# Second attention of a gated two-layer block: the output bias added by a TensorE product instead of a GpSimd addition, and GpSimd's small factor product in front of its rounding

## The chip, the cores and the metric

The kernel runs on one core of one Trainium2 chip. The metric is the device time of one execution in microseconds. Before the change three runs gave 405.77, 406.14 and 408.43 us, a median of 406.14 us. Engines are called by the profile's names: PE is TensorE (PEld its weight load), DVE is VectorE, ACT is ScalarE, POOL is GpSimd, SP is SyncE, which issues the DMAs.

## The reference, cut to what matters

The whole block has two layers, each a cross attention and a feed-forward part, each behind a normalisation and a gate:

```
x = x + tanh(g_xattn[0]) * L0_xattn(ctx, norm(x), mask, ...)
x = x + tanh(g_ffn[0])   * L0_ffn(norm(x), ...)        # 16 experts, top-k tokens
x = x + tanh(g_xattn[1]) * L1_xattn(norm(x), ctx, ctx, ...)
x = x + tanh(g_ffn[1])   * L1_ffn(norm(x), ...)        # ternary weights, 8-bit activations
```

The change lies in the last two lines. With 32 sequences of 64 rows and 128 channels, they compute

```
wq, wk, wv = q @ wq_w.T + wq_b, k @ wk_w.T + wk_b, v @ wv_w.T + wv_b   # 16 heads of 8
probs = softmax(wq . wk / sqrt(8));  attn = probs . wv
y = attn @ wo_w.T + wo_b                                 # wo_b: the bias that moves
x = x + tanh(g) * y
h = layernorm(x) * gamma + beta
scale = 127 / max(|h|);  hq = round(h * scale)           # act_quant, a row at a time
u = (hq @ w1q.T) / (scale * sw) + b1;  g = gelu(u)       # then the same again with w2, b2
```

The gate is already folded into the prepared weight and bias, so the kernel only has to add `attn @ w + bias` to x. The bias wo_b is a row of 128 numbers that is the same for all tokens.

## The kernel before, in words

The tokens are 2048 rows, cut into 16 tiles (t = 0 to 15) of 128 rows by 128 channels, float32; the tile with x is `xs[:, t, :]`. The function `attention_ffn` computes the second layer for all 16 tiles, and its work starts where the first layer's experts end. Each engine has its own queue, strictly in the written order, and the engines meet only at semaphores. So the order of the work is written out by hand, engine by engine: first a short loop that adds the expert outputs up, then a loop over steps s in which every engine treats several tiles at once, each at another stage, and then a hand-ordered tail for the last tiles and the second half of the feed-forward part.

In a turn of the loop PE does, in this order, for different tiles: `mix` (probabilities by values, 8 small products in each of two halves, j=1 into bank `b_y` and j=0 into bank `b_m`, L1533), `turn_context` (L1474), `turn_attention` (transposes the divided attention rows, L1545), `turn_input` (L1480), `up` (first feed-forward product, L1566), `scores` (L1504), `turn_norm` (L1559), `probs_T` (eight transposes, L1519), `out_proj` (attention rows by output weight, into `b_y`, L1550) and `project` (query, key, value, L1490 to L1493).

DVE does `row_stats` (L1896), `norm_largest` (L1905), `attend` (reciprocal of the sums L1878, then the two products into `b_att`, L1883), `norm_factors` (L1910 gives the bound, semaphore h_bound; L1913 its reciprocal, semaphore h_fine), `row_moments` (L1900), `hidden` (L1920), `row_max` (L1861), `output` (L1892: x is set to the product in `b_y` plus `xb`), `shift` (L1866) and `invert` (L1874).

POOL does `add_bias` (L1352: `xb` = x + bias, x and bias both in SBUF), `norm_round` (L1374: multiplies by the fine factor and rounds, waits for h_fine), `norm_back` (L1380: a 128x1 product that keeps the factor back to full scale, waits for h_bound), `normalise` (L1339), `inverse_root` (L1356, L1359), `norm` (L1366 to L1369) and `spread_keys` (L1346). In the tail POOL also does `add_bias_2` (L1387) and `hidden_back` (L1393), DVE `hidden_largest` (L1925), `hidden_bound` (L1930) and `hidden_round` (L1939).

ACT moves PSUM results to SBUF (`b_oT` L1727 is the transposed attention that out_proj reads) and does the exponential (L1717) and the gelu (L1737). In the profile the names of tiles carry the prefix b_.

Of the kernel before, what the change touches and what calls it, by code (L numbers as in the profile page):

```python
# [22 lines left out]
ALU = mybir.AluOpType  # L23
# [7 lines left out]
P = 128  # L31


def wait(eng, sem, count):

    if isinstance(count, int) and count <= 0:
        return
    eng.wait_ge(sem, count)
# [27 lines left out]
def exists(t, tiles):  # L66

    return not isinstance(t, int) or 0 <= t < tiles
# [1169 lines left out]
def attention_ffn(nc, v, o_tiles):  # L1238
# [6 lines left out]
    xs, cs, mrow, nrow, neghalf, ident, quad = (v[n] for n in "xs cs mrow nrow neghalf ident quad".split())  # L1245
# [12 lines left out]
    with ExitStack() as ph, nc.Block() as block:  # L1258
        def sb(name, shape, dt=F32):
            return ph.enter_context(nc.sbuf_tensor("b_" + name, shape, dt))  # L1260
# [4 lines left out]
        def sem(name):  # L1265
# [14 lines left out]
        rs = sb("rs", [P, 2, HP, 2])  # L1280
        att = sb("att", [P, 2, HP, 2, DH])
        oT = sb("oT", [P, 2, P])
        xb = sb("xb", [P, 2, D])
        hn = sb("hn", [P, 2, D])
        hr = sb("hr", [P, 2, D])
        hT = sb("hT", [P, 2, P], BF16)
# [17 lines left out]
        p_prob, p_mix, p_out = (p_m, p_t), (p_m, p_y), (p_t, p_m)  # L1304
        (zeroed, ready, xn_ready, cT_done, xT_done, cT_ready, xT_ready, qkv_done, k_ready, q_ready, v_ready, k4_ready,
         scored, maxed, shifted, exped, pT_done, prT_ready, mixed, inverse, att_ready, aT_done, oT_ready, y_done,
         xb_ready, x_new) = (
            sem(n) for n in ("zeroed", "ready", "xn_ready", "cT_done", "xT_done", "cT_ready", "xT_ready", "qkv_done",
                             "k_ready", "q_ready", "v_ready", "k4_ready", "scored", "maxed", "shifted", "exped",
                             "pT_done", "prT_ready", "mixed", "inverse", "att_ready", "aT_done", "oT_ready", "y_done",  # L1310
                             "xb_ready", "x_new"))
        (stats_ready, mv_ready, var_ready, rstd_ready, hn_chain, hn_ready, h_max, h_bound, h_fine, h_back, hr_ready,
         hT_done, hT_ready, up_done, hid_ready, gelu_done, g_max, g_bound, g_fine, g_back, g_rounded, gT_done,
         gT_ready, down_done, xb2_ready, x_done) = (
# [13 lines left out]
        @block.sync  # L1328
        def _(sp):
            for t in range(NT // 2):  # L1330
                sp.wait_ge(x_done, t + 1)
                sp.dma_start(o_tiles[:, 2 * t:2 * t + 2, :], xs[:, 2 * t:2 * t + 2, :]).then_inc(stored, 16)
            sp.wait_ge(stored, 16 * (NT // 2))

        @block.gpsimd
        def _(pool):
# [5 lines left out]
            def spread_keys(t, tp):  # L1342
# [3 lines left out]
                    last = nc.gpsimd.tensor_tensor(k4[:, tp, b], ksb[:, tp, b].unsqueeze(1).to_broadcast([P, G, S]),  # L1346
                                                   quad[:].unsqueeze(2).to_broadcast([P, G, S]), ALU.mult)
                last.then_inc(k4_ready, 1)

            def add_bias(t, tp):  # L1350
                wait(pool, x_new, t - 1)
                nc.gpsimd.tensor_tensor(xb[:, tp, :], xs[:, t, :], rows[:, 2, :], ALU.add).then_inc(xb_ready, 1)  # L1352

            def inverse_root(t):
                pool.wait_ge(mv_ready, t + 1)
                nc.gpsimd.tensor_tensor(nrow[:, t, :], mrow[:, t, 0:4:2], mrow[:, t, 1:4:2], ALU.subtract)\  # L1356
                    .then_inc(var_ready, 1)
                pool.wait_ge(var_ready, t + 1)
                nc.gpsimd.tensor_tensor(nrow[:, t, 1:2], nrow[:, t, 1:2], neghalf[:, 0:1], ALU.pow)\  # L1359
                    .then_inc(rstd_ready, 1)  # L1360

            def norm(t, tp):
                pool.wait_ge(rstd_ready, t + 1)
                wait(pool, hr_ready, t - 1)
                step = Steps(pool, hn_chain, 2 * t)
                step(nc.gpsimd.tensor_scalar(hn[:, tp, :], xs[:, t, :], nrow[:, t, 0:1], nrow[:, t, 1:2],  # L1366
                                             ALU.add, ALU.mult))
                step(nc.gpsimd.tensor_tensor(hn[:, tp, :], hn[:, tp, :], rows[:, 4, :], ALU.mult))
                nc.gpsimd.tensor_tensor(hn[:, tp, :], hn[:, tp, :], rows[:, 5, :], ALU.add).then_inc(hn_ready, 1)  # L1369

            def norm_round(t, tp):
                pool.wait_ge(h_fine, t + 1)
                wait(pool, hT_done, t - 1)
                nc.gpsimd.tensor_scalar(hr[:, tp, :], hn[:, tp, :], fine[:, 0, t % 4], MAGIC, ALU.mult, ALU.add)\  # L1374
                    .then_inc(hr_ready, 1)

            def norm_back(t):
                pool.wait_ge(h_bound, t + 1)
                wait(pool, hid_ready, t - 3)
                nc.gpsimd.tensor_tensor(back_[:, 0, t % 4], top[:, 0, t % 4], wback[:, 0:1], ALU.mult).then_inc(h_back, 1)  # L1380
# [9 lines left out]
            def hidden_back(j):  # L1390
                pool.wait_ge(g_bound, j + 1)
                r = slice(2 * j, 2 * j + 2)
                nc.gpsimd.tensor_tensor(back2[:, r], top2[:, r], wback[:, 1:2].to_broadcast([P, 2]),  # L1393
                                        ALU.mult).then_inc(g_back, 1)
# [8 lines left out]
            pool.wait_ge(ready, 1)  # L1403
            pool.wait_ge(rooted, NT)
            for s in range(NT + 1):
                if exists(s - 3, NT):
                    add_bias(s - 3, (s - 3) % 2)
                if exists(s - 5, NT):
                    norm_round(s - 5, (s - 5) % 2)
                    norm_back(s - 5)  # L1410
                if exists(s + 3, NT):
                    normalise(s + 3)
                if exists(s - 4, NT):
                    inverse_root(s - 4)
                    norm(s - 4, s % 2)
                if s >= 1 and exists(s, NT):
                    spread_keys(s, s % 2)
            inverse_root(13)
            add_bias(14, 0)
            norm(13, 1)  # L1420
            norm_round(12, 0)
            norm_back(12)
            add_bias(15, 1)
            add_bias_2(0)
            inverse_root(14)
            norm_round(13, 1)
            norm_back(13)
            norm(14, 0)
            add_bias_2(1)
            hidden_back(0)  # L1430
# [3 lines left out]
            inverse_root(15)  # L1434
            add_bias_2(4)
            norm(15, 1)
            norm_round(14, 0)
            norm_back(14)
            add_bias_2(5)
            hidden_back(2)  # L1440
            add_bias_2(6)
            hidden_back(3)
            add_bias_2(7)
            hidden_back(4)
            norm_round(15, 1)
            norm_back(15)
            hidden_back(5)
            hidden_back(6)
            hidden_back(7)
# [2 lines left out]
        def _(pe):  # L1452
# [94 lines left out]
            def out_proj(t, tp):  # L1547
                pe.wait_ge(oT_ready, t + 1)
                wait(pe, hid_ready, t - 2)
                nc.tensor.matmul(p_y[:, 0:D], oT[:, tp, :], w_c[:, 3, :], start=True, stop=True).then_inc(y_done, 1)  # L1550

            def turn_norm(t, tp):
                pe.wait_ge(hr_ready, t + 1)
# [266 lines left out]

        @block.vector
        def _(dve):
            nc.vector.memset(vals[:], 0.0).then_inc(zeroed, 1)
            nc.vector.tensor_copy(wback[:, 0:1], wmean[:, 0:1])
            nc.vector.tensor_scalar(wback[:, 1:2], wmean[:, 1:2], gates[:, 3:4], None, ALU.mult).then_inc(ready, 1)
            dve.wait_ge(zeroed, 1)
            for a in range(2):
                nc.vector.memset(vals[a * S:(a + 1) * S, :, :, :, a, DH:DH + 1].rearrange("p x b n o -> p (x b n) o"), 1.0)\
                    .then_inc(zeroed, 1)
# [58 lines left out]

            def output(t, tp):
                dve.wait_ge(y_done, t + 1)  # L1890
                dve.wait_ge(xb_ready, t + 1)
                nc.vector.tensor_tensor(xs[:, t, :], p_y[:, 0:D], xb[:, tp, :], ALU.add).then_inc(x_new, 1)  # L1892

            def row_stats(t, tp):
                dve.wait_ge(x_new, t + 1)
# [171 lines left out]
```

## Time and profile before

| | before |
|---|---|
| median of 3 runs (lowest to highest) | 406.14 us (405.77 to 408.43) |
| profiled execution: its own time | 406.96 us |
| its span, first to last instruction | 404.5 us |
| mean granted TensorE clock | 0.97 of full speed |
| busy: PE, PEld, DVE, ACT, POOL | 371.9, 274.4, 323.2, 258.3, 221.4 us |
| the second layer's loop over tiles | about 286 to 371 us of the span |
| the hand-ordered tail | about 371 us to the end |

The profiled execution took 2.5 us more than its span, and 0.8 us more than the median of the runs. A float32 product of 128x128 by 128x128 stands in the trace as two matmul records, a float32 transpose as one. Matmul records overlap, so what a product costs a busy PE is read from start to start and not from the duration of one record. A few records of L1566 are missing from the trace; where they are, PE shows a gap called "issue".

### The profile page before, as it was taken

The numbers are of one execution on the slowest core, as the hardware profiler recorded it, in microseconds if no ns is written. First come the engines' busy times: TensorE is split into PE (matmuls) and PEld (weight loads), VectorE is DVE, ScalarE is ACT, GpSimd is POOL, SyncE is SP. The second block draws the span as 40 slices with busy tenths as digits, with TensorE's granted clock in tenths as the row PEclk, the third lists the DMA queues.
The fourth block names the chain that finished last, engine by engine and source line by source line (L and its number), as shares of the span: only waits on it lengthen the run. The fifth ranks groups of instructions, "written<-read, shape, count | busy, mean of one in ns | idle before, by whom it ended". The sixth has DMA issues, their size and how long they took to land. (4 is left out here: it accounts for less than half of the span.)

```text
span 404.5 us, 10543 instructions
## 1 busy us (share of the span) xinstructions
PE 371.9 (92%) x3599; PEld 274.4 (68%) x3612; DVE 323.2 (80%) x911; ACT 258.3 (64%) x514; POOL 221.4 (55%) x388
## 2 busy tenths in 40 slices
PE   7799999999999999999999999999799888886675
PEld 7356766676666666678756888787577777765464
DVE  4889999899989989888482888464647888887896
ACT  2578767777777777776654222345357777777784
POOL 4574577766666666663231000076438888877760
PEclk9999999999999999999999999999769999999689
DMA  5979999900000000000000000000000000000003
GB/s 152 258 145 115 138 128 125 93 2 2 2 2 1 2 2 2 2 0 5 0 2 0 2 0 2 1 2 2 0 2 2 2 2 4 2 2 2 2 13 92
DMA packets 61283, 13.27 MB, mean 33 GB/s; under 512 B 51488, under 2 KB 60592, under 8 KB 61232
## 3 DMA queue, kind: packets, MB, share of 16 engines
q1 hardware_dynamic: 59776, 11.94, 21.4%
q10 hardware_dynamic: 1328, 0.66, 0.6%
q8 instruction: 30, 0.49, 0.5%
q14 instruction: 21, 0.17, 0.2%
q0 software_dynamic: 128, 0.00, 0.0%
HBM read 11.55 MB, written 1.05 MB: 31 GB/s over the span
## 5 line engine op out<-in xcount | busy, mean ns | idle before, releaser
L398 POOL TENSOR_TENSOR a_rn<-a_ssq,neghalf 128x8 f32<-128x8 f32 x48 | 79.0, 1655 | 29.1 <-DVE a_ssq L999 24.5
L999 DVE TENSOR_REDUCE a_ssq<-q_home 128x8 f32<-128x512 f32 x48 | 32.3, 673 | 6.5 <-ACT q_home L784 6.4
L90 POOL TENSOR_TENSOR nrow<-mrow 128x2 f32<-128x2 f32 x32 | 6.3, 198 | 55.8 <-DVE mrow L86 55.5
L487 PE MATMUL a_x<-wkv_a,a_kvT 128*128 128x512 f32 x64 | 34.5, 621 | 0.9 <-ACT kv_home L790 0.8
L790 ACT ACTIVATE kv_home<-a_x,maskcol 128x512 f32<-128x512 f32 x32 | 21.9, 684 | 18.4 <-PE a_x L487 18.4
L1346 POOL TENSOR_TENSOR b_k<-b_ksb,quad 128x256 f32<-128x256 f32 x32 | 19.0, 614 | 15.5 <-ACT b_ksb L1697 15.5
L1861 DVE TENSOR_REDUCE b_mx<-b_s 128x16 f32<-128x1024 f32 x16 | 19.6, 1224 | 6.3 <-PE b_s L1504 6.3
L414 POOL TENSOR_TENSOR a_yr<-a_ymv,eps_row 128x1 f32<-128x1 f32 x16 | 3.1, 191 | 37.8 <-DVE a_ymv L1042 37.8
L1018 DVE TENSOR_REDUCE a_mx<-a_s 128x4 f32<-128x512 f32 x32 | 21.9, 685 | 2.0 <-PE a_s L513 1.9
L802 ACT ACTIVATE kv_home<-a_m,cols 128x512 f32<-128x512 f32 x32 | 22.0, 686 | 0.8 <-PE a_m L501 0.6
L532 PE MATMUL a_m<-kv_home,p_home 128*64 128x65 f32 x512 | 22.0, 228 | 0.3 <-ACT p_home L812 0.3
L513 PEld LDWEIGHTS a_s<-kv_home,q_home 64*64 64x64 f32 x512 | 13.9, 132 | 12.1 <-issue 12.1
L1025 DVE TENSOR_TENSOR p_home<-a_s,a_mx 128x512 f32<-128x512 f32 x32 | 21.8, 682 | 0.0
L523 PEld LDWEIGHTS a_m<-ident,p_home 128*128 128x128 f32 x128 | 14.6, 140 | 10.2 <-issue 10.0
L501 PEld LDWEIGHTS a_m<-ident,q_home 128*128 128x128 f32 x128 | 15.3, 140 | 9.2 <-issue 7.9
L532 PEld LDWEIGHTS a_m<-kv_home,p_home 128*64 128x64 f32 x512 | 17.7, 137 | 5.5 <-issue 5.5
L812 ACT COPY p_home<-a_m 128x512 f32<-128x512 f32 x32 | 18.7, 586 | 4.0 <-PE a_m L523 4.0
L551 PEld LDWEIGHTS a_y<-wo_a,p_home 128*128 128x128 f32 x128 | 16.6, 191 | 6.4 <-issue 6.2
L92 POOL TENSOR_TENSOR nrow<-nrow,neghalf 128x1 f32<-128x1 f32 x32 | 18.8, 588 | 2.5
L523 PE MATMUL a_m<-ident,p_home 128*128 128x128 f32 x128 | 20.1, 280 | 0.0
L807 ACT ACTIVATE p_home<-p_home 128x512 f32<-128x512 f32 x32 | 19.9, 622 | 0.3 <-DVE p_home L1025 0.3
L501 PE MATMUL a_m<-ident,q_home 128*128 128x128 f32 x128 | 19.3, 273 | 0.4 <-DVE q_home L1011 0.4
(294 smaller groups left out, 1150.7 us busy)
## 6 DMA issues: line engine op xcount, KB each, us to landing
w_gu<-in_L_ffn_Wg_dram SPq DMA_DIRECT2D x4, 512.0 KB, 9.2
w_gu<-in_L_ffn_Wu_dram SPq DMA_DIRECT2D x4, 512.0 KB, 11.2
w_d<-in_L_ffn_Wd_dram SPq DMA_DIRECT2D x8, 256.0 KB, 8.5
out_dram<-xs SPq DMA_DIRECT2D x8, 128.0 KB, 1.8
xs<-in_x_dram SPq DMA_DIRECT2D x1, 640.0 KB, 11.2
cs<-in_ctx_dram SPq DMA_DIRECT2D x1, 640.0 KB, 11.2
wkv_a<-in_L_xattn_Wkv_dram SPq DMA_DIRECT2D x1, 512.0 KB, 7.5
nat<-in_L_ffn_w_dram SPq DMA_DIRECT2D x2, 256.0 KB, 3.1
```

The source lines that it names most:

```text
L398: nc.gpsimd.tensor_tensor(rn[:, tp, i, :], ssq[:, tp, i, :], neghalf[:, 0:H0], ALU.pow)\
L487: nc.tensor.matmul(p_x[:], kvT[:, tp, b * 2 * S:(b + 1) * 2 * S], wkv_a[:, INNER:2 * INNER], start=True, stop=True).then_inc(vproj_done, 1)
L501: last = nc.tensor.transpose(p_m[b][:, h * P:(h + 1) * P], kn[:, b, h * P:(h + 1) * P], ident[:])
L523: last = nc.tensor.transpose(p_m[a][:, h * P:(h + 1) * P], pr[:, a, h, :], ident[:])
L532: last = nc.tensor.matmul(p_m[a][b * S:(b + 1) * S, h * W:(h + 1) * W], prT[:, a, h, b * S:(b + 1) * S], vaug[:, tp, b, 2 * h + a, :], sta ...
L790: nc.scalar.activation(vaug[:, tp, b, :, 0:DH0], p_x[:].rearrange("p (h d) -> p h d", h=H0), ACT.Copy, scale=maskcol[:, 2 * t + b:2 * t + ...
L802: nc.scalar.activation(kT[:, tp, b, :, :], p_m[b][:].rearrange("p (h k) -> p h k", h=HP), ACT.Copy, scale=cols[:, 4:5]).then_inc(kT_ready, 1)
L807: nc.scalar.activation(pr[:, a], pr[:, a], ACT.Exp).then_inc(exped, 1)
L999: nc.vector.tensor_reduce(ssq[:, tp, i, :], sq[:, i, :].rearrange("p (h d) -> p h d", h=H0), AX.X, ALU.add).then_inc(reduced, 1)
L1018: nc.vector.tensor_reduce(mx[:, a, :], p_s[a][:].rearrange("p (h k) -> p h k", h=HP), AX.X, ALU.max)\
L1025: nc.vector.tensor_tensor(pr[:, a], s3, mx[:, a, :].unsqueeze(2).to_broadcast([P, HP, P]), ALU.subtract).then_inc(shifted, 1)
L1861: nc.vector.tensor_reduce(mx[:, tp], s4, AX.X, ALU.max).then_inc(maxed, 1)
```

## The change

Four things change, all in `attention_ffn`.

`out_proj` issues two products into the same bank instead of one. The first multiplies a constant tile `first_row` (128x128, ones in its first row and zeros elsewhere) by the tile that holds the bias in every row, and so writes the bias to all 128 rows; the second is the old product and is added on top (start=False).

`add_bias` and its tile `xb`, its semaphore xb_ready and its 16 calls on POOL are gone. DVE's `output` adds the bank to x in place and waits for one semaphore less.

On POOL `norm_back` stands in front of `norm_round` of the same tile, in the loop and in the tail.

DVE fills `first_row` by two memsets at the start of `attention_ffn`.

```diff
@@ -1280,7 +1280,7 @@
         rs = sb("rs", [P, 2, HP, 2])
         att = sb("att", [P, 2, HP, 2, DH])
         oT = sb("oT", [P, 2, P])
-        xb = sb("xb", [P, 2, D])
+        first_row = sb("first_row", [P, P])
         hn = sb("hn", [P, 2, D])
         hr = sb("hr", [P, 2, D])
         hT = sb("hT", [P, 2, P], BF16)
@@ -1304,11 +1304,11 @@
         p_prob, p_mix, p_out = (p_m, p_t), (p_m, p_y), (p_t, p_m)
         (zeroed, ready, xn_ready, cT_done, xT_done, cT_ready, xT_ready, qkv_done, k_ready, q_ready, v_ready, k4_ready,
          scored, maxed, shifted, exped, pT_done, prT_ready, mixed, inverse, att_ready, aT_done, oT_ready, y_done,
-         xb_ready, x_new) = (
+         x_new) = (
             sem(n) for n in ("zeroed", "ready", "xn_ready", "cT_done", "xT_done", "cT_ready", "xT_ready", "qkv_done",
                              "k_ready", "q_ready", "v_ready", "k4_ready", "scored", "maxed", "shifted", "exped",
                              "pT_done", "prT_ready", "mixed", "inverse", "att_ready", "aT_done", "oT_ready", "y_done",
-                             "xb_ready", "x_new"))
+                             "x_new"))
         (stats_ready, mv_ready, var_ready, rstd_ready, hn_chain, hn_ready, h_max, h_bound, h_fine, h_back, hr_ready,
          hT_done, hT_ready, up_done, hid_ready, gelu_done, g_max, g_bound, g_fine, g_back, g_rounded, gT_done,
          gT_ready, down_done, xb2_ready, x_done) = (
@@ -1346,10 +1346,6 @@
                     last = nc.gpsimd.tensor_tensor(k4[:, tp, b], ksb[:, tp, b].unsqueeze(1).to_broadcast([P, G, S]),
                                                    quad[:].unsqueeze(2).to_broadcast([P, G, S]), ALU.mult)
                 last.then_inc(k4_ready, 1)
-
-            def add_bias(t, tp):
-                wait(pool, x_new, t - 1)
-                nc.gpsimd.tensor_tensor(xb[:, tp, :], xs[:, t, :], rows[:, 2, :], ALU.add).then_inc(xb_ready, 1)
 
             def inverse_root(t):
                 pool.wait_ge(mv_ready, t + 1)
@@ -1403,11 +1399,9 @@
             pool.wait_ge(ready, 1)
             pool.wait_ge(rooted, NT)
             for s in range(NT + 1):
-                if exists(s - 3, NT):
-                    add_bias(s - 3, (s - 3) % 2)
                 if exists(s - 5, NT):
+                    norm_back(s - 5)
                     norm_round(s - 5, (s - 5) % 2)
-                    norm_back(s - 5)
                 if exists(s + 3, NT):
                     normalise(s + 3)
                 if exists(s - 4, NT):
@@ -1416,15 +1410,13 @@
                 if s >= 1 and exists(s, NT):
                     spread_keys(s, s % 2)
             inverse_root(13)
-            add_bias(14, 0)
             norm(13, 1)
+            norm_back(12)
             norm_round(12, 0)
-            norm_back(12)
-            add_bias(15, 1)
             add_bias_2(0)
             inverse_root(14)
+            norm_back(13)
             norm_round(13, 1)
-            norm_back(13)
             norm(14, 0)
             add_bias_2(1)
             hidden_back(0)
@@ -1434,16 +1426,16 @@
             inverse_root(15)
             add_bias_2(4)
             norm(15, 1)
+            norm_back(14)
             norm_round(14, 0)
-            norm_back(14)
             add_bias_2(5)
             hidden_back(2)
             add_bias_2(6)
             hidden_back(3)
             add_bias_2(7)
             hidden_back(4)
+            norm_back(15)
             norm_round(15, 1)
-            norm_back(15)
             hidden_back(5)
             hidden_back(6)
             hidden_back(7)
@@ -1547,7 +1539,8 @@
             def out_proj(t, tp):
                 pe.wait_ge(oT_ready, t + 1)
                 wait(pe, hid_ready, t - 2)
-                nc.tensor.matmul(p_y[:, 0:D], oT[:, tp, :], w_c[:, 3, :], start=True, stop=True).then_inc(y_done, 1)
+                nc.tensor.matmul(p_y[:, 0:D], first_row[:], rows[:, 2, :], start=True, stop=False)
+                nc.tensor.matmul(p_y[:, 0:D], oT[:, tp, :], w_c[:, 3, :], start=False, stop=True).then_inc(y_done, 1)
 
             def turn_norm(t, tp):
                 pe.wait_ge(hr_ready, t + 1)
@@ -1820,10 +1813,12 @@
 
         @block.vector
         def _(dve):
+            nc.vector.memset(first_row[:], 0.0)
             nc.vector.memset(vals[:], 0.0).then_inc(zeroed, 1)
             nc.vector.tensor_copy(wback[:, 0:1], wmean[:, 0:1])
             nc.vector.tensor_scalar(wback[:, 1:2], wmean[:, 1:2], gates[:, 3:4], None, ALU.mult).then_inc(ready, 1)
             dve.wait_ge(zeroed, 1)
+            nc.vector.memset(first_row[0:1, :], 1.0)
             for a in range(2):
                 nc.vector.memset(vals[a * S:(a + 1) * S, :, :, :, a, DH:DH + 1].rearrange("p x b n o -> p (x b n) o"), 1.0)\
                     .then_inc(zeroed, 1)
@@ -1888,8 +1883,7 @@
 
             def output(t, tp):
                 dve.wait_ge(y_done, t + 1)
-                dve.wait_ge(xb_ready, t + 1)
-                nc.vector.tensor_tensor(xs[:, t, :], p_y[:, 0:D], xb[:, tp, :], ALU.add).then_inc(x_new, 1)
+                nc.vector.tensor_tensor(xs[:, t, :], p_y[:, 0:D], xs[:, t, :], ALU.add).then_inc(x_new, 1)
 
             def row_stats(t, tp):
                 dve.wait_ge(x_new, t + 1)
```

PE, one turn of the loop around out_proj, before (b_oT is the transposed attention, w_c the weights, b_k, b_y, b_m and b_t PSUM banks):

```order
L1519 MATMUL b_m<-ident,b_pr 128x128 x3
L1550 MATMUL b_y<-w_c,b_oT 128x128 [waits b_hid_ready,b_oT_ready]
L1490 MATMUL b_k<-b_cT,w_c 128x128 [waits b_k_ready,b_oT_ready,b_q_ready,b_hT_ready,b_v_ready,b_xT_ready,b_cT_ready]
L1491 MATMUL b_k<-b_xT,w_c 128x128
L1493 MATMUL b_k<-w_c,b_cT 128x128 x2
L1533 MATMUL b_y<-b_vals,b_prT 64x18 [waits b_hid_ready,b_x_new,b_att_ready,b_v_ready,b_prT_ready]
```

PE at the same place, now:

```order
L1511 MATMUL b_m<-ident,b_pr 128x128 x3
L1542 MATMUL b_y<-rows,b_first_row 128x128 [waits b_hid_ready,b_oT_ready]
L1543 MATMUL b_y<-w_c,b_oT 128x128
L1482 MATMUL b_k<-b_cT,w_c 128x128 [waits b_k_ready,b_oT_ready,b_q_ready,b_hT_ready,b_v_ready,b_xT_ready,b_cT_ready]
L1483 MATMUL b_k<-b_xT,w_c 128x128
L1485 MATMUL b_k<-w_c,b_cT 128x128 x2
L1525 MATMUL b_y<-b_vals,b_prT 64x18 [waits b_hid_ready,b_x_new,b_att_ready,b_v_ready,b_prT_ready]
```

One product more stands between the transposes of the probabilities and the projections, and the two waits of out_proj now stand in front of the new product.

POOL, one turn of the loop, before:

```order
L1346 TENSOR_TENSOR b_k<-b_ksb,quad 128x256
L1352 TENSOR_TENSOR b_xb<-xs,rows 128x128 [waits b_x_new]
L1374 TENSOR_SCALAR b_hr<-b_hn,b_fine 128x128 [waits b_hT_done,b_h_fine]
L1380 TENSOR_TENSOR b_back_<-b_top,b_wback 128x1 [waits b_hid_ready,b_h_bound]
L1339 TENSOR_SCALAR b_xn<-xs,nrow 128x128 [waits b_xT_done]
L1356 TENSOR_TENSOR nrow<-mrow 128x2 [waits b_mv_ready]
```

POOL at the same place, now:

```order
L1346 TENSOR_TENSOR b_k<-b_ksb,quad 128x256
L1376 TENSOR_TENSOR b_back_<-b_top,b_wback 128x1 [waits b_hid_ready,b_h_bound]
L1370 TENSOR_SCALAR b_hr<-b_hn,b_fine 128x128 [waits b_hT_done,b_h_fine]
L1339 TENSOR_SCALAR b_xn<-xs,nrow 128x128 [waits b_xT_done]
L1352 TENSOR_TENSOR nrow<-mrow 128x2 [waits b_mv_ready]
```

The addition into b_xb is gone (in the new numbering L1352 is another line), and the 128x1 product stands ahead of the rounding.

## Rows read from the trace of the kernel before

**Rows 1.** The page, part 1: busy time of each engine, share of the span, instructions.

```profile
PE 371.9 (92%) x3599; PEld 274.4 (68%) x3612; DVE 323.2 (80%) x911; ACT 258.3 (64%) x514; POOL 221.4 (55%) x388
```

**Rows 2.** Timeline of PE, one turn (start us, us, instruction, idle before).

```profile
329.07 0.33 PE L1545 MATMUL b_k<-ident,b_att 128*128 128x128 f32 x1 [0.44 <-DVE b_att L1883]
...
331.36 0.39 PE L1550 MATMUL b_y<-w_c,b_oT 128*128 128x128 f32 x2
331.58 0.39 PE L1490 MATMUL b_k<-b_cT,w_c 128*128 128x128 f32 x2
...
332.57 0.65 PE L1533 MATMUL b_y<-b_vals,b_prT 128*64 128x18 f32 x16
333.06 0.63 PE L1533 MATMUL b_m<-b_vals,b_prT 128*64 128x18 f32 x16
...
334.38 0.33 PE L1545 MATMUL b_k<-ident,b_att 128*128 128x128 f32 x1 [0.44 <-DVE b_att L1883]
```

**Rows 3.** Timeline of DVE, the same turn.

```profile
330.50 1.22 DVE L1861 TENSOR_REDUCE b_mx<-b_s 128x16 f32<-128x1024 f32 x1
331.79 0.29 DVE L1892 TENSOR_TENSOR xs<-b_y,b_xb 128x128 f32<-128x128 f32 x1
331.99 1.21 DVE L1866 TENSOR_TENSOR b_pr<-b_s,b_mx 128x1024 f32<-128x1024 f32 x1
333.26 0.21 DVE L1874 RECIPROCAL b_rs<-b_y 128x8 f32<-128x8 f32 x1
...
333.55 0.27 DVE L1905 TENSOR_REDUCE b_top<-b_hn 128x1 f32<-128x128 f32 x1
333.73 0.21 DVE L1878 RECIPROCAL b_rs<-b_m 128x8 f32<-128x8 f32 x1
...
334.25 0.14 DVE L1910 TENSOR_SCALAR b_top<-b_top 128x1 f32<-128x1 f32 x1
```

**Rows 4.** Chain of waits: out_proj of the first tile (start us, us, what).

```profile
299.21 0.43 PE b_y L1550 x2
```

**Rows 5.** Timeline of PE, summing the expert outputs: two products added into one bank.

```profile
262.38 0.61 PE L1463 MATMUL b_s<-ws_t,kv_home 128*128 128x128 f32 x4
262.92 0.44 PE L1467 MATMUL b_s<-b_turned 128*64 128x128 f32 x4
```

**Rows 6.** Timeline of POOL, the same turn of the loop.

```profile
333.12 1.18 POOL L1346 TENSOR_TENSOR b_k<-b_ksb,quad 128x256 f32<-128x256 f32 x2 [0.36 <-ACT b_ksb L1697]
334.26 0.45 POOL L1352 TENSOR_TENSOR b_xb<-xs,rows 128x128 f32<-128x128 f32 x1
334.70 0.37 POOL L1374 TENSOR_SCALAR b_hr<-b_hn,b_fine 128x128 f32<-128x128 f32 x1
```

**Rows 7.** Timeline of all engines in the tail, about the last two tiles.

```profile
376.34 0.46 POOL L1352 TENSOR_TENSOR b_xb<-xs,rows 128x128 f32<-128x128 f32 x1
...
380.35 0.77 PE L1550 MATMUL b_y<-w_c,b_oT 128*128 128x128 f32 x2 [0.31 <-DVE b_hid L1920]
...
381.07 1.60 POOL L1387 TENSOR_TENSOR xs<-xs,rows 128x256 f32<-128x256 f32 x2
381.24 0.28 DVE L1892 TENSOR_TENSOR xs<-b_y,b_xb 128x128 f32<-128x128 f32 x1
381.44 0.64 DVE L1939 TENSOR_SCALAR b_hid<-b_hid,b_fine 128x512 f32<-128x512 f32 x1
...
382.21 0.49 DVE L1930 TENSOR_SCALAR b_top<-b_top 128x2 f32<-128x2 f32 x1
...
382.70 0.13 DVE L1930 TENSOR_SCALAR b_top<-b_top 128x2 f32<-128x2 f32 x1
```

**Rows 8.** A stretch: us, busy time (count) of PE, PEld, DVE, ACT, POOL, granted clock, DMA, GB/s.

```profile
286.00:302.00 16.00, 13.47 (x125) 10.88 (x127) 7.05 (x11) 8.29 (x22) 4.68 (x10) 0.57 0.01 2
```

**Rows 9.** Timeline of PE: the same instruction of two early turns.

```profile
295.53 0.48 PE L1545 MATMUL b_k<-ident,b_att 128*128 128x128 f32 x1 [0.29 <-DVE b_att L1883]
...
303.10 0.33 PE L1545 MATMUL b_k<-ident,b_att 128*128 128x128 f32 x1 [0.44 <-DVE b_att L1883]
```

## The prediction, before the changed kernel had run

> **What bounds the kernel now.** I read the page first: PE is busy for 92% of the span, DVE for 80%, POOL for 55% [rows 1]. That points at PE, but a share over the whole span doesn't say what an added PE product costs in the one loop where it is added. So I read the timeline of a single turn of that loop, engine by engine, and the chain of waits beside it.
>
> A turn lasts 5.31 us: `turn_attention` starts at 329.07 and again at 334.38 [rows 2]. PE has work without a hole from the scores to the end of the two halves of `mix`; what it waits for is 0.44 us each turn, always for DVE's `b_att`. So the turn closes like this: PE ends mix, DVE divides (L1878, L1883), PE transposes the result, and PE goes on through scores, transposes, out_proj, projections and mix again.
>
> Is it PE or DVE that sets the pace in that ring? DVE shows almost no idle time there either, so I compare starts with ends. The record of out_proj ends at 331.36 + 0.39 = 331.75 and DVE's `output` starts at 331.79. The first half of mix ends at 332.57 + 0.65 = 333.22 and `invert` starts at 333.26. The second half ends at 333.06 + 0.63 = 333.69 and the next reciprocal starts at 333.73 [rows 2, 3]. Three times DVE starts exactly 0.04 us behind PE. Two of these starts lie later than DVE's own queue would put them: `row_max` ended at 331.72 and `shift` at 333.20, so `output` and `invert` came 0.07 and 0.06 us after the end of what stood before, while a DVE instruction that waits for nothing starts before the recorded end of the one ahead of it (333.55 + 0.27 = 333.82, next start 333.73) [rows 3]. DVE therefore waits for PE, by little (0.07 + 0.09, some 0.16 us at `output`, and about as much again at `invert`). PE sets the pace, and a longer PE turn is a longer turn.
>
> **The added product, in the loop.** A 128x128 float32 product costs a busy PE its distance from start to start: out_proj starts at 331.36 and the next product at 331.58, 0.22 us [rows 2]. (Its two records last 0.39 together because they overlap the next.) The new product has the same shape, and it stands in the continuous part. That it adds into the same bank costs no extra by the nearest rows: four records that add into one bank went from 262.38 to 262.92, 0.54 us [rows 5], and the four records of the projections that don't take the same time in front of 332.57. The loop runs out_proj for tiles 0 to 13. Thirteen of them run at the full clock: 13 x 0.22 = 2.9 us. Tile 0 falls into the stretch at a mean granted clock of 0.57 [rows 8], that is mostly at the lower level, and its product cost 0.43 us on the chain [rows 4]: +0.43. (If the clock rises at the same moment as before, only about 0.22 of it is left, since work pushed past that moment runs fast.) Loop: +3.3 us. The ends: nothing, if PE isn't what binds (the first rival), and 14 x 0.39 = 5.5 us, if the new product cost the whole recorded length of the old one. I take 0.22, since the very same product stands in that row.
>
> **The removed addition on POOL.** 16 x 0.46 us = 7.3 us of POOL's work go [rows 6]. In the loop they stand between `spread_keys` and `norm_round`. POOL is idle there for 0.36 us a turn, waiting for ACT's keys, which come from PE's projections [rows 6], so POOL is not what the turn waits for. The 0.46 us become idle time: 0 gained.
>
> **The swap on POOL.** `norm_back` now waits first, for the bound, which DVE finishes at 334.25 + 0.14 = 334.39 [rows 3]. Before, the addition covered that wait. The 128x1 product behind it is a short one, and the rounding, which starts at 334.70 now [rows 6], has 0.3 us of room for it. So with the cover gone the rounding is not delayed, and nothing is gained. What queues behind is `normalise`, which is needed only in the next turn: 0. DVE's `output` reads x instead of xb, with one wait less and the same shape: 0. Two memsets at the start of the part have 128 columns each, like the 0.29 us of `output`, so 0.6 us at most, and DVE waits for PE's first sum behind them: 0.
>
> **The tail.** Tile 14's product is hidden, since PE waits for ACT before and after it and DVE is in a long reduction meanwhile. Tile 15's isn't. It runs at the lower clock (its pair took 0.77 us against 0.39 [rows 2, 7]), where a product costs 0.43 [rows 4]; the old one ended at about 381.1, the new pair at 381.55, and DVE's `output`, now at 381.24, moves to 381.6: +0.35, and everything behind it on DVE. Against this stands a stall in the same place. DVE's L1930 on 128x2 takes 0.13 us at 382.70 but 0.49 at 382.21, when it ends at 382.70 just as POOL's two additions do at 381.07 + 1.60 = 382.67; L1939 at 381.44 ends at 382.08, 0.2 us after the first of them [rows 7]. The Trainium skill, "SBUF — State Buffer" (section "SBUF: two separate sides"), says that a DVE instruction in a two-port mode and a GpSimd instruction hold one port pair as an exclusive lock, so that the loser waits for the whole instruction; these rows agree. With the addition at 376.34 gone, POOL's queue, which is full from there on, comes 0.41 us earlier (the next instruction stood 0.41 behind it), and its last addition ends at 382.26. DVE, 0.35 later, then finds POOL done at L1930 and saves those 0.35 us, but L1939 now meets POOL's second addition and ends at about 382.45. From 382.70 the sequence is 0 to 0.1 us later than before: **tail +0.1**, between -0.5 and +0.6, since each further meeting of the two engines can cost or save 0.2 to 0.5.
>
> **Sum.** 0.43 + 2.9 + 0.1 = +3.4 us. The profiled execution (span 404.5, its own time 406.96) would become 410.4; it lies 0.8 above the median of the runs, so the forecast against the median of 406.14 is **409.5 us**, 0.8% slower.
>
> **Rivals.**
>
> *DVE sets the pace (not slower), chance 0.12.* If the ends of PE's records, which the profile models, are late by 0.2 us, DVE's queue binds the turn and the new product falls into PE's waiting time of 0.44 us. It decides from 0.22 us of slack in `row_max` to `invert`. Then only tile 0 and the tail show: 406.1 + 0.4 at most, and with a better meeting with POOL in the tail (-0.5) 405.9. For it: DVE has hardly a gap of 0.1 us in those rows. Against: three starts that follow PE by the same 0.04 us. The skill's port rule would favour this rival, as 0.46 us of POOL's two-input additions go each turn; but in the loop L1910 stands right beside L1352 and takes 0.14 us [rows 3, 6], its undisturbed time, so there is nothing to save.
>
> *The product costs more than its spacing (slower), chance 0.07.* Its own weights, loaded each turn, and a bank that is still being written could break the stream. At its whole recorded length of 0.39 a turn: 406.1 + 5.5 + 0.1 = 411.7. Against: the 0.54 us of four records, adding or not [rows 5].
>
> *The clock (slower), chance 0.12.* TensorE is at its lower level of 1.2 GHz in most of 286 to 302 [rows 8] and again in the tail, where tile 15's pair ran [rows 7], each time after PE had stood waiting for other engines. Nothing in front of 286 changes, so the first fall stays; when it rises again, and where the second fall meets a tail that begins 3.3 us later, can shift. One turn more at 1.2 GHz costs as much as the difference between the turn from 295.53 to 303.10 and a full-speed one, 7.6 - 5.3 = 2.3 us [rows 2, 9]: 411.8. The Trainium skill, "TensorE: Matmul & The Clock Gate" (Part 4), says that transposes don't count as activity for this gate. By that rule the added product, which is no transpose, could only help to keep the clock up; no run here shows yet that it does, and I give it no time.
>
> *As forecast, chance 0.69*, with its own range of 408.7 to 410.5: 0.2 for the first tile, 0.5 for the tail, 0.3 for the medians.
>
> **Range and chances.** The forecast and part of the clock case below 411.2, and from the first rival's side down to 407.3, hold 8 in 10: **407.3 to 411.2**. This kernel's runs tell a difference from none at about 1%, here 4.1 us, so the border to "slower" is 410.2 and to "faster" 402.1. Slower by over 1%: 0.07, most of the clock case (0.10) and some of the forecast's (0.08): 0.25. Faster by over 1%: 0.01. Within 1%: 0.74.
>
> **What would show it.** In the new trace the turn should be 5.53 us, with the two products of out_proj 0.22 apart, `output` still 0.04 behind the second one's end, and PE's wait for `b_att` still 0.44. POOL's wait for ACT's keys should grow from 0.36 to about 0.9, since it loses 0.46 and the turn grows. A turn of 5.31 with a wait of 0.22 on PE would prove the first rival, a product spacing over 0.3 the second, a stretch of half clock longer than before the third. The forecast is wrong in the tail if DVE's L1930 at the old 382.21 still takes 0.4 us or more.

## The result: slower by 0.6%, and the profile after

In 20 runs each the changed kernel takes 406.66 us (406.11 to 410.44) and the one before 405.51 (402.62 to 408.43). The ratio is **1.0064, 95% interval 1.0045 to 1.0083**, that is +2.6 us (1.8 to 3.4) on 405.5. The forecast was +3.4 us on a median of 406.14, 409.5 us. That median of three was itself 0.6 above the one of 20 runs; the measured ratio on it gives 1.0064 x 406.14 = 408.7 us, inside the range of 407.3 to 411.2. As a difference, +2.6 stands against +3.4. The two medians as they stand lie closer together, 1.15 us or 1.0028, and 406.66 by itself is below the range: single executions of either kernel scatter by more than the change (the lowest and highest of the kernel before are 5.8 us apart), and the ratio, taken run by run in their order, is the figure that has an interval.

The page of the profile after, busy time and granted clock:

```profile
PE 376.0 (93%) x3644; PEld 277.1 (69%) x3644; DVE 323.5 (80%) x913; ACT 257.8 (64%) x514; POOL 215.1 (53%) x372
...
PEclk9999999999999999999999999999899999998599
```

PE has 4.1 us more than before and POOL 6.3 less, with 16 instructions fewer [rows 1]. The span is 404.5 us, the same as before to a tenth. Read alone, that would say that the change costs nothing. A turn of the loop says otherwise. PE in the changed kernel (start us, us, instruction, idle before), the turn that answers to [rows 2]:

```profile
332.43 0.33 PE L1537 MATMUL b_k<-ident,b_att 128*128 128x128 f32 x1 [0.44 <-DVE b_att L1878]
...
334.72 0.39 PE L1542 MATMUL b_y<-rows,b_first_row 128*128 128x128 f32 x2
334.94 0.39 PE L1543 MATMUL b_y<-w_c,b_oT 128*128 128x128 f32 x2
335.17 0.39 PE L1482 MATMUL b_k<-b_cT,w_c 128*128 128x128 f32 x2
...
336.15 0.65 PE L1525 MATMUL b_y<-b_vals,b_prT 128*64 128x18 f32 x16
336.64 0.63 PE L1525 MATMUL b_m<-b_vals,b_prT 128*64 128x18 f32 x16
...
337.96 0.33 PE L1537 MATMUL b_k<-ident,b_att 128*128 128x128 f32 x1 [0.44 <-DVE b_att L1878]
```

337.96 - 332.43 is 5.53 us, against 5.31. From `turn_attention` to out_proj 2.29 us pass in both kernels (331.36 - 329.07 before); the two products stand 0.22 apart, the projection behind them is 0.45 later than the start of the first instead of 0.22, and the wait for `b_att` is still 0.44. The whole product has gone into the turn. DVE in the same turn:

```profile
335.37 0.29 DVE L1886 TENSOR_TENSOR xs<-b_y,xs 128x128 f32<-128x128 f32 x1 [0.28 <-PE b_y L1543]
335.57 1.21 DVE L1861 TENSOR_TENSOR b_pr<-b_s,b_mx 128x1024 f32<-128x1024 f32 x1
336.85 0.21 DVE L1869 RECIPROCAL b_rs<-b_y 128x8 f32<-128x8 f32 x1
...
337.32 0.20 DVE L1873 RECIPROCAL b_rs<-b_m 128x8 f32<-128x8 f32 x1
```

`output` starts 0.04 us behind the end of the second product (334.94 + 0.39 = 335.33), `invert` 0.05 and its second part 0.05 behind the halves of mix. The releases of [rows 3] are the same, but in front of `output` DVE now shows 0.28 us idle: more slack, as it must be where PE sets the pace. POOL, answering to [rows 6]:

```profile
336.70 1.18 POOL L1346 TENSOR_TENSOR b_k<-b_ksb,quad 128x256 f32<-128x256 f32 x2 [0.77 <-ACT b_ksb L1690]
338.05 0.19 POOL L1376 TENSOR_TENSOR b_back_<-b_top,b_wback 128x1 f32<-128x1 f32 x1 [0.16 <-DVE b_top L1904]
338.28 0.37 POOL L1370 TENSOR_SCALAR b_hr<-b_hn,b_fine 128x128 f32<-128x128 f32 x1
```

Its wait for the keys went from 0.36 to 0.77, with 0.16 more in front of `norm_back`, where the addition used to stand. The rounding starts 0.32 us after `turn_attention` (338.28 - 337.96), exactly as before (334.70 - 334.38).

**Why the spans are equal.** I set the starts of `turn_attention` of both profiles beside each other:

| stretch | before | after | difference |
|---|---|---|---|
| start of the span to tile 0's | 295.53 | 294.55 | -0.98 |
| first turn | 7.57 | 5.16 | -2.41 |
| the next 12 turns | 63.48 | 66.19 | +2.71 |
| tile 13's to tile 15's | 11.96 | 12.64 | +0.68 |
| from there to the end | 25.96 | 25.96 | 0.00 |

The first two lines aren't the change's, all but the 0.22 us that tile 0's product adds to the first turn: in front of 286 us the program is unchanged but for two memsets, and the granted clock of the stretch differs (0.50 from 288 to 300 us before, 0.73 and 0.84 in 288 to 292 and 292 to 296 after, then 1.00). The same window as [rows 8], of the kernel after (us, busy time and count of PE, PEld, DVE, ACT, POOL, granted clock, DMA, GB/s), and its two early turns, as in [rows 9]:

```profile
286.00:302.00 16.00, 12.76 (x169) 10.31 (x168) 9.53 (x18) 11.18 (x29) 7.16 (x15) 0.89 0.01 2
```

```profile
294.55 0.33 PE L1537 MATMUL b_k<-ident,b_att 128*128 128x128 f32 x1 [0.45 <-DVE b_att L1878]
...
299.71 0.33 PE L1537 MATMUL b_k<-ident,b_att 128*128 128x128 f32 x1 [0.44 <-DVE b_att L1878]
```

The one profiled execution of the kernel before had an unlucky stretch at half clock there, 0.57 against 0.89, and one first turn of 7.57 us that the eight other profiles show as 4.7 to 5.4. Those 3.4 us hide the 3.4 us of the loop and the last tiles. The fourth line has tile 13's product and the second fall of the clock, at about 372 us after and 377 before. The other profiles part the two: the same stretch takes 11.96, 12.05 and 12.04 us in the three kernels without an added product, 12.18 in the kernel with a zero product and in the changed kernel profiled again, and 12.40 with two zero products. So about 0.2 of the 0.68 is the product, and the rest belongs to this one execution.

### The profile page after: what moved, and what is told of

Same layout as the page of the kernel before. It is cut to its first block and busy times, and to the rows that moved or that the text cites. A ratio compares the mean times of both kernels' runs of the same rounds, so it can differ in the third digit from the quotient of the medians.

```text
span 404.5 us, 10590 instructions
## 1 busy us (share of the span) xinstructions
PE 376.0 (93%) x3644; PEld 277.1 (69%) x3644; DVE 323.5 (80%) x913; ACT 257.8 (64%) x514; POOL 215.1 (53%) x372
```

## Experiments

Theory P: PE sets the pace of the loop, a product in its continuous part costs its start-to-start distance, and what POOL does costs nothing. Rivals: the cost comes from the operand or bank and not from the place (the whole record), from the swap on POOL, or DVE sets the pace. All but the last kernel ran in five rounds with the kernel before beside them. The first four shared one chip (kernel before 404.8 us), the other three another (404.4).

### One zero product, POOL as before

`zero_row` is a 128x128 tile of zeros, filled once by DVE, so the product adds nothing to the result.

```diff
-  nc.tensor.matmul(p_y[:, 0:D], oT[:, tp, :], w_c[:, 3, :], start=True, stop=True).then_inc(y_done, 1)
+  nc.tensor.matmul(p_y[:, 0:D], zero_row[:], rows[:, 2, :], start=True, stop=False)
+  nc.tensor.matmul(p_y[:, 0:D], oT[:, tp, :], w_c[:, 3, :], start=False, stop=True).then_inc(y_done, 1)
```

> The kernel before with one more product in out_proj: a tile of zeros by the bias tile, added into the same bank; GpSimd keeps its addition, its order and its own time. Theory (PE sets the turn, the product is the whole price): the turn goes from 5.31-5.32 to 5.54 us, +0.22 in each of 13 turns plus the two slow tiles, in all +3.0 to +3.6 us over the kernel before, ratio 1.007 to 1.009. Rival 1 (DVE sets the turn, the product falls into PE's wait): turn 5.32, ratio 1.000 to 1.001. Rival 2 (the removal on GpSimd gives part back in the changed kernel): this kernel is slower than the changed one by 0.3 us or more.

Measured: 406.49 us, ratio 1.0056 (1.0024 to 1.0087). The ratio came out below the 1.007 to 1.009 that I had expected, but its interval reaches into that range. PE of this kernel:

```profile
331.00 0.33 PE L1546 MATMUL b_k<-ident,b_att 128*128 128x128 f32 x1 [0.44 <-DVE b_att L1886]
...
333.30 0.39 PE L1551 MATMUL b_y<-rows,b_zero_row 128*128 128x128 f32 x2
333.52 0.39 PE L1552 MATMUL b_y<-w_c,b_oT 128*128 128x128 f32 x2
...
336.55 0.33 PE L1546 MATMUL b_k<-ident,b_att 128*128 128x128 f32 x1 [0.44 <-DVE b_att L1886]
```

5.55 us a turn, the changed kernel's to a hundredth or two, with all of POOL's additions still there. The product alone makes the loop's loss. The ratios can't say whether this kernel is slower than the changed one by a few tenths of a microsecond, as the rival of the removal on POOL asked: the interval here alone is 1.3 us wide to each side. The turns say that nothing of it is in the loop; the tail follows below.

### Two zero products

The same edit with the zero product twice.

> The same with two added zero products. PE sets the turn: turn 5.76 us, twice the difference of the kernel with one (+6 to +7 us, ratio 1.015 to 1.017). If part of the first product had been covered by slack, the second one costs more than the first; if the product costs only where the queue stalls, both cost less than 0.22 a turn.

Measured: 410.66 us, ratio 1.0156 (1.0113 to 1.0198), which is +6.3 us. Its PE:

```profile
330.15 0.33 PE L1546 MATMUL b_k<-ident,b_att 128*128 128x128 f32 x1 [0.44 <-DVE b_att L1887]
...
332.44 0.39 PE L1551 MATMUL b_y<-rows,b_zero_row 128*128 128x128 f32 x2
332.67 0.39 PE L1552 MATMUL b_y<-rows,b_zero_row 128*128 128x128 f32 x2
332.89 0.39 PE L1553 MATMUL b_y<-w_c,b_oT 128*128 128x128 f32 x2
...
335.91 0.33 PE L1546 MATMUL b_k<-ident,b_att 128*128 128x128 f32 x1 [0.44 <-DVE b_att L1887]
```

The turn is 5.76, again 0.22 more, and twelve turns take 68.95 us: 5.47 over the 63.48 of before, 2 x 12 x 0.228. With 0.44 each for tiles 0 and 13 that makes 6.35 us, what the ratio says. The cost of a turn grows in proportion from the first product, so there was no slack that the first one used up.

### The changed kernel without its bias product

The output bias is left out: POOL doesn't add it, and PE has no product for it.

```diff
-  nc.tensor.matmul(p_y[:, 0:D], first_row[:], rows[:, 2, :], start=True, stop=False)
-  nc.tensor.matmul(p_y[:, 0:D], oT[:, tp, :], w_c[:, 3, :], start=False, stop=True).then_inc(y_done, 1)
+  nc.tensor.matmul(p_y[:, 0:D], oT[:, tp, :], w_c[:, 3, :], start=True, stop=True).then_inc(y_done, 1)
```

> The changed kernel without its first product in out_proj, so the output bias of the second attention is left out; GpSimd's addition is gone and its order swapped. Theory: GpSimd isn't waited for in the loop, so the turn stays 5.31-5.32 us and GpSimd's wait for the keys grows from 0.36 to about 0.8; only the tail can move, by -0.5 to +0.1 us: ratio 0.998 to 1.000. Rival (GpSimd's two-input additions hold up DVE in the loop): turn 5.2 us or less, ratio below 0.996.

Measured: 403.03 us, ratio 0.9986 (0.9955 to 1.0016). PE, then POOL:

```profile
331.08 0.33 PE L1537 MATMUL b_k<-ident,b_att 128*128 128x128 f32 x1 [0.44 <-DVE b_att L1877]
...
336.40 0.33 PE L1537 MATMUL b_k<-ident,b_att 128*128 128x128 f32 x1 [0.44 <-DVE b_att L1877]
```

```profile
335.14 1.18 POOL L1346 TENSOR_TENSOR b_k<-b_ksb,quad 128x256 f32<-128x256 f32 x2 [0.54 <-ACT b_ksb L1689]
```

The turn is back at 5.32 us. Taking 0.46 us a turn off POOL gives a turn nothing; it turns up as waiting time: 0.54 here and 0.16 in front of `norm_back`, together 0.70 against 0.36, where I had expected about 0.8 in one place.

### The kernel before with the swap alone

```diff
-  norm_round(s - 5, (s - 5) % 2)
   norm_back(s - 5)
+  norm_round(s - 5, (s - 5) % 2)
```

(and so for tiles 12 to 15 in the tail)

> The kernel before with GpSimd's small factor product in front of the rounding, nothing else. Theory: the addition in front still covers the wait, so the rounding starts about 0.15 us later (behind the product) and has 0.3 us of room or more before PE turns it: turn 5.31-5.32, ratio 0.999 to 1.001. Rival: PE's transposition of the rounded rows waits, turn 5.4 or more, ratio 1.002 or more.

Measured: 404.27 us, ratio 1.0005 (0.9975 to 1.0035). POOL of this kernel, whose `turn_attention` stands at 332.50:

```profile
332.38 0.45 POOL L1352 TENSOR_TENSOR b_xb<-xs,rows 128x128 f32<-128x128 f32 x1
332.80 0.19 POOL L1380 TENSOR_TENSOR b_back_<-b_top,b_wback 128x1 f32<-128x1 f32 x1
332.96 0.37 POOL L1374 TENSOR_SCALAR b_hr<-b_hn,b_fine 128x128 f32<-128x128 f32 x1
```

The rounding starts 0.46 after `turn_attention` and so 0.14 later than before, since here the addition still stands in front. The next `turn_attention` is at 337.81, a turn of 5.31: the delay is absorbed. In the changed kernel it doesn't even arise.

### The same product in PE's wait instead

If P holds, PE's 0.44 us of waiting for `b_att` would take both products (2 x 0.22) for nothing. They need another bank there, since `b_y` holds the sums of mix at that time: 128 columns of `b_s` behind the scores are free between DVE's `shift` and the next scores. DVE's `output` and `row_stats` follow behind `attend`. Tiles 0 to 12 go this way, 13 to 15 the old one. PE's waits move with them: out_proj waits for DVE's `shift`, the next scores that go into the same bank wait for `output`, and `up` and `mix` of the early tiles no longer do. The core of the edit, against the changed kernel:

```diff
+  EARLY = NT - 3
+  def y_out(t):
+      return p_s[:, 0, 4 * S:4 * S + D] if t < EARLY else p_y[:, 0:D]
...
   if s >= 2 and exists(s, NT):
       turn_context(s)
+  if exists(s - 4, NT):
+      out_proj(s - 4, s % 2)
   if exists(s - 3, NT):
       turn_attention(s - 3, (s - 3) % 2)
...
-  if exists(s - 3, NT):
+  if s - 3 == EARLY:
       out_proj(s - 3, (s - 3) % 2)
...
   attend(s - 2, s % 2)
+  output(s - 3, (s - 3) % 2)
   norm_factors(s - 4)
+  row_stats(s - 3, (s - 3) % 2)
```

> The changed kernel with both products of out_proj taken out of PE's continuous part for tiles 0 to 12: they go into PE's wait for the divided attention rows, right behind the next tile's mix, and write into unused columns of a scores bank; DVE's addition and the row statistics move behind the division, where DVE waits for the up product. Theory (a product costs 0.22 us a turn only where PE has no hole; PE still sets the turn): the wait of 0.44 us takes both products (0.44), the turn falls from 5.54 to 5.10 us, 4 to 5.5 us less than the changed kernel and 1.5 to 3 less than the kernel before: ratio 0.992 to 0.996. Rival (DVE, which has 0.46 us of waiting in a turn and now does the same work in another order, becomes the bound): turn 5.3 or more, ratio 1.000 or more.

Measured: **400.96 us, ratio 0.9925 (0.9894 to 0.9956)**, faster than both kernels (the changed one takes 406.5 on this chip, below). PE, then DVE:

```profile
328.51 0.39 PE L1553 MATMUL b_s<-rows,b_first_row 128*128 128x128 f32 x2
328.73 0.39 PE L1554 MATMUL b_s<-w_c,b_oT 128*128 128x128 f32 x2
329.11 0.33 PE L1545 MATMUL b_k<-ident,b_att 128*128 128x128 f32 x1
...
334.15 0.33 PE L1545 MATMUL b_k<-ident,b_att 128*128 128x128 f32 x1
```

```profile
329.15 0.29 DVE L1900 TENSOR_TENSOR xs<-b_s,xs 128x128 f32<-128x128 f32 x1
```

A turn is 5.04 us and no wait is left in front of L1545, which still starts 0.69 us behind the end of mix, as before: PE does the two products while DVE divides. From 319.03 to 359.36 there are eight such turns, in which PE is busy for 39.11 of 40.33 us.

### The same place, bias added by POOL

The same edit on the kernel before, so one product in the wait and POOL's addition kept.

> The kernel before (bias added by GpSimd) with its one product of out_proj moved in the same way. Theory: turn 5.10 us as well, since the hole has room for one product or two; ratio 0.991 to 0.995, no different from the version with two products by more than 0.2%. If the hole is too small for two, this one is faster by up to 0.22 us a turn (2.6 us). Rival (DVE bound): 5.3 or more, ratio 1.000 or more.

Measured: 401.08 us, ratio 0.9925 (0.9891 to 0.9959).

```profile
328.03 0.39 PE L1561 MATMUL b_s<-w_c,b_oT 128*128 128x128 f32 x2
328.63 0.33 PE L1553 MATMUL b_k<-ident,b_att 128*128 128x128 f32 x1 [0.22 <-DVE b_att L1897]
...
333.76 0.33 PE L1553 MATMUL b_k<-ident,b_att 128*128 128x128 f32 x1 [0.22 <-DVE b_att L1897]
```

Here half of the wait is left, 0.22 us, which is the room that the bias product fills in the kernel above; the medians differ by 0.1 us. So the same product that costs 0.22 us a turn in the changed kernel costs nothing in the wait in front of `turn_attention`, and the gain of 0.75% comes with the old product's new place, whoever adds the bias. (DVE's `output` and some waits moved along with it and weren't tried alone.) (These two rows are 5.13 apart, most turns 5.04; eight of them, from 318.53 to 359.07, have a mean of 5.07. A turn fell by 0.24 to 0.27 us and not by the 0.22 of the one product that left the stream. The rest stands between `turn_attention` and `scores`, 0.63 us from start to start in the kernel before, at 329.07, 0.58 in the turn from 324.07 of the kernel with both products in the wait, and 0.67 in the turn of 5.13 here. `up` stands in between, and the edit drops one of its waits. In the first three turns, which have no `up` yet, the turn fell by 0.21 or 0.22: 4.72, 4.72 and 4.91 here against 4.94, 4.94 and 5.12 in the swap's kernel. So the rest belongs to `up`; whether to its dropped wait wasn't tested.)

### The changed kernel again

> The changed kernel once more, as a yardstick on the same chip as its two relatives: ratio 1.004 to 1.008, turn 5.54 us. A different stretch of lower clock behind the sum of the expert outputs moves its span by up to 2.4 us and not its full-speed turns.

Measured in three rounds: 406.5 us, ratio 1.0046 (1.0016 to 1.0076), a turn of 5.54. Its profiled span is 406.9 us, 2.4 more than that of the same kernel in the profile above, although the clock in 286 to 302 is 1.00 this time. In this execution the clock fell earlier, to 0.51 and 0.64 of full in 200 to 204 and 204 to 208 us, a part that the change doesn't touch, and tile 0's `turn_attention` starts at 297.30 instead of 294.55.

## Why the prediction was right, point by point

**What bounds the loop: right.** The distance of 0.04 us between PE's ends and DVE's starts named PE, and the kernels agree: 0, 1 and 2 added products give turns of 5.32, 5.53 to 5.55 and 5.76 us with the wait for `b_att` unchanged at 0.44. The rival that DVE sets the pace asked for a turn of 5.31 with a wait of 0.22; that appeared in no kernel with the product at the old place. The rival of a whole record (0.39 a turn, +5.5) is out as well: two products together cost 5.47 over twelve turns, where two records of 0.39 would have cost 9.4.

**The product in the loop: right for twelve turns, too much for the first.** Forecast 13 x 0.22 = 2.9 at full clock; the trace has 2.71 for twelve turns, and the profiles above put another 0.2 into the stretch from tile 13 to tile 15 (12.18 against about 12.0). Tile 0's term was mis-sized: I took 0.43, since the profile before had the lower clock there. The first turn at full clock is 5.16 with the product (the changed kernel, in both profiles) and 4.94 without (the swap alone and the kernel without bias): 0.22. The lower clock in that place belonged to that one execution, as far as the record shows: its mean granted clock of 0.970 is matched or undercut by only two of the 55 executions of the kernel before whose clock was noted in the experiments (without one that took 1985 us), 0.966 and 0.970, at 410.23 and 408.34 us; the others have 0.973 to 0.983.

**POOL's removed addition and the swap, 0 each in the loop: right.** The kernel without the bias product has both of them (0.9986), the other the swap alone (1.0005), each with 1 inside its interval. These intervals are 1.2 us wide to each side, so what carries the point is the turns, 5.32 and 5.31. POOL's wait for the keys was forecast as about 0.9; it is 0.77 and 0.16 in two places, 0.93 together.

**The tail, +0.1: right in sum as far as two profiles can say, with one step that depends on chance.** All engines of the changed kernel, answering to [rows 7]:

```profile
380.44 0.76 PE L1542 MATMUL b_y<-rows,b_first_row 128*128 128x128 f32 x2 [0.41 <-DVE b_hid L1914]
380.45 1.42 POOL L1383 TENSOR_TENSOR xs<-xs,rows 128x256 f32<-128x256 f32 x2
...
381.00 0.63 PE L1543 MATMUL b_y<-w_c,b_oT 128*128 128x128 f32 x2
381.67 0.29 DVE L1886 TENSOR_TENSOR xs<-b_y,xs 128x128 f32<-128x128 f32 x1 [0.25 <-PE b_y L1543]
381.88 0.48 DVE L1933 TENSOR_SCALAR b_hid<-b_hid,b_fine 128x512 f32<-128x512 f32 x1
...
382.48 0.15 DVE L1924 TENSOR_SCALAR b_top<-b_top 128x2 f32<-128x2 f32 x1
...
382.69 0.14 DVE L1924 TENSOR_SCALAR b_top<-b_top 128x2 f32<-128x2 f32 x1
```

`output` comes at 381.67 (forecast 381.6, before 381.24), and the small DVE instruction on `b_top` takes 0.15 instead of 0.49, as forecast; the second one starts at 382.69 against 382.70. I had POOL 0.41 us earlier. It is 0.62 earlier (380.45 against 381.07): beside the addition, the swap gives POOL about 0.14 there, since `norm_back` of tile 12 now runs while POOL waits for the fine factor, and I had put the swap at 0. So its two additions end at 381.87 and DVE's long instruction behind `output` meets nothing: 0.48 us, where I had expected it to be held. The second profile of the changed kernel shows the case that I had forecast:

```profile
383.13 1.41 POOL L1383 TENSOR_TENSOR xs<-xs,rows 128x256 f32<-128x256 f32 x2
384.05 0.77 DVE L1933 TENSOR_SCALAR b_hid<-b_hid,b_fine 128x512 f32<-128x512 f32 x1
...
384.95 0.14 DVE L1924 TENSOR_SCALAR b_top<-b_top 128x2 f32<-128x2 f32 x1
```

There the long instruction starts 0.49 us before POOL's additions end (383.13 + 1.41 = 384.54) and takes 0.77. Which of the two happens hangs on a few tenths of a microsecond, and not on the kernel. The kernel with the zero product and POOL's addition kept is the counter-test:

```profile
379.69 1.59 POOL L1388 TENSOR_TENSOR xs<-xs,rows 128x256 f32<-128x256 f32 x2
379.84 0.29 DVE L1895 TENSOR_TENSOR xs<-b_y,b_xb 128x128 f32<-128x128 f32 x1 [0.25 <-PE b_y L1552]
380.05 0.64 DVE L1942 TENSOR_SCALAR b_hid<-b_hid,b_fine 128x512 f32<-128x512 f32 x1
...
380.81 0.49 DVE L1933 TENSOR_SCALAR b_top<-b_top 128x2 f32<-128x2 f32 x1
```

The small instruction is held until POOL's two additions end (380.81 + 0.49 = 381.30 against 379.69 + 1.59 = 381.28), and the long one ends at 380.69, 0.2 us after the middle of the two. The small instruction in this place takes 0.48 or 0.49 in all five kernels that keep POOL's addition, and 0.14 or 0.15 in the four profiles without it. The last stretch, from tile 15's `turn_attention` to the end, in us:

| added products | POOL's addition kept | removed |
|---|---|---|
| none | 25.96 (before), 26.30 (swap) | 25.62 (no bias) |
| one | 26.74 (zero product) | 25.96, 26.04 (changed, twice) |
| two | 27.16 (two zero products) | |

So the product costs something like 0.3 to 0.8 us here, the missing addition gives back about as much, and the two nearly cancel, as the forecast had it with 0.35 each. The single values are good to a few tenths only, since the clock fell at different times in the tails of all these profiles; of the 0.7 to 0.8 us between the zero product's kernel and the changed one, the two held instructions show 0.16 + 0.34 = 0.5.

**The sum.** 0.22 + 2.71 + 0.22 + 0 = 3.15 us, 1.0078, inside the interval of 1.0045 to 1.0083. The forecast's 3.4 had 0.2 too much for tile 0 and 0.1 for the tail. That is the small part of the 2.8 us between 409.5 and the measured median of 406.66. Another 0.6 is the start from a high median of three. The middle of the interval is 0.5 us below what the traces add up to, and the plain medians lie 1.4 us closer together than the ratio says; no run here says whether these two are more than chance. The terms are confirmed turn by turn; that the time came out inside the range rests on the ratio, not on the median by itself.

**The clock: as big as the change, but in the profile's execution rather than in the kernel.** I gave it a chance as a change of the kernel (+2.3). The granted clock of the stretch 286 to 302, over all nine profiles, is 0.57 in the kernel before, 0.89 in the changed one, the one without bias, the one with two zero products and both with the product in the wait, and 1.00 in the zero product, the swap and the changed kernel again: the same kernel shows two values, so the value isn't the edit's. Nor does 1.00 there mean a faster run: in the changed kernel again and in the swap alone the clock fell between 196 and 208 us instead, and tile 0's turn began later than in the zero product's profile, where it fell in neither place (297.30 and 296.19 against 293.13).

## What to carry to other kernels

Find the pacing engine of a loop by who starts a fixed few hundredths of a microsecond behind whom; then price a product by its start-to-start distance in the place where it stands, and what is taken off an engine that waits at zero. If the pacing engine has a wait in the same turn, work whose inputs are ready by then and that fits into it was free here: the same product cost 0.22 us a turn in the stream and nothing in the wait. Moving the old product there gave 0.75%, with the bias on PE or on POOL, while trading POOL's addition for a product in the stream cost 0.6%. Compare two profiles turn by turn, never by their spans, when the differences in question are below 1%.

## What the runs showed of the hardware

- One turn at the lower of the clock's two levels, 1.2 GHz for most of it, took 7.57 us and the same turn 4.94 at 2.4 GHz. Those 2.6 us are as large as the whole change, and the stretch isn't tied to the kernel: two executions of the changed kernel had 0.89 and 1.00 of full clock in the same 16 us, and the one with 1.00 had its fall some 90 us earlier.
- A float32 128x128 product added into a bank right behind another costs 0.22 us at full clock, the first of two as much as the second, whatever the operand: ones in one row, zeros or data.
- A DVE instruction of two elements a partition, 0.13 to 0.15 us by itself, took 0.48 or 0.49 beside POOL's additions of two SBUF operands in all five kernels where it met them, and 0.14 or 0.15 in the four profiles where these had ended. A later one took 0.70 to 0.72 beside them in all nine. A DVE instruction of 128x512 took 0.48 by itself and 0.59 to 0.77 where it was held.
